# Routed experts of one mixture-of-experts layer: another order of the experts, and another way of adding the base

## The reference, cut to what matters

```
x = x + gnn(layernorm(x), edges)            # graph layer
xn = layernorm(x)
shared = sum over 2 shared experts:  silu(xn @ sWg[e]) * (xn @ sWu[e]) @ sWd[e]
gate = top 6 of 64 softmax(xn @ Wr), made to sum to 1, else 0
routed = sum over e in 0..63: (silu(xn @ Wg[e]) * (xn @ Wu[e]) @ Wd[e]) * gate[:, e]
out = x + (shared + routed + xn)            # all weights 512 x 512, f32
```

## Time and profile before

| | |
|---|---|
| median of 3 runs | 756.45 us (755.75 to 759.19) |
| the profiled execution, its own time | 754.59 us |
| its span, first to last instruction | 752.8 us |
| PE busy | 696.7 us (93%) |
| DVE, ACT, POOL busy | 251.4, 221.1, 174.0 us |
| DMA | 236.33 MB, 314 GB/s over the span |
| TensorE clock granted | 0.988 of full speed, mean |

### The profile page before, as it was taken

The page is one execution under the profiler, slowest core; times in us unless marked ns, Lnnn a source line. Parts: engine busy times, 40 slices in busy tenths (PEclk is TensorE's granted clock), DMA queues, the critical chain, the costliest instruction groups (busy, mean ns, idle before and its releaser), DMA issues. The chain is left out here.

```text
span 752.8 us, 17410 instructions
## 1 busy us (share of the span) xinstructions
PE 696.7 (93%) x6982; PEld 474.1 (63%) x6982; DVE 251.4 (33%) x795; ACT 221.1 (29%) x536; POOL 174.0 (23%) x157
## 2 busy tenths in 40 slices
PE   3689999899999999999999999999999999999960
PEld 2467777566766666555666666655567777777740
DVE  6975625775112432221212111122323222221000
ACT  5733323512332222212222222221222333233320
POOL 4000000012222322323322222223333332232202
PEclk9999999999999999999999999999999999999996
DMA  9925112447999999999999999999999999999962
GB/s 270 410 86 224 39 74 81 156 145 261 362 372 343 388 389 382 386 393 385 378 389 383 381 399 380 385 393 385 385 382 375 371 368 370 367 375 373 381 165 28
DMA packets 63408, 236.33 MB, mean 314 GB/s; under 512 B 7323, under 2 KB 7359, under 8 KB 51550
## 3 DMA queue, kind: packets, MB, share of 16 engines
q1 hardware_dynamic: 51764, 211.33, 73.3%
q0 software_dynamic: 10144, 20.56, 11.7%
q10 hardware_dynamic: 1418, 3.30, 1.2%
HBM read 222.32 MB, written 12.83 MB: 312 GB/s over the span
## 5 line engine op out<-in xcount | busy, mean ns | idle before, releaser
L461 POOL DMA_INDIRECT xg<-x_tab,idx_sb x64 | 69.9, 1092 | 375.5 <-DVE idx_sb L1048 193.6
L1528 PE MATMUL ps<-ring,xT 128*64 128x256 f32 x1296 | 148.4, 380 | 0.2 <-DVE hs L1107 0.2
L473 POOL DMA_INDIRECT out<-ysb,idx_sb x64 | 93.3, 1458 | 189.6 <-issue 112.7
L1528 PEld LDWEIGHTS ps<-ring,xT 128*64 128x64 f32 x1296 | 93.6, 137 | 46.7 <-issue 1.1
L1041 DVE TENSOR_REDUCE gates<-ps 128x1 f32<-128x3 f32 (+1 forms) x62 | 10.0, 162 | 331.3 <-PE ps L1434 330.6
L707 ACT ACTIVATE ysb<-ps 64x256 f32<-64x256 f32 x64 | 24.1, 377 | 201.4 <-PE ps L1528 192.9
L1528 PE MATMUL ps<-ring,hTj 128*64 128x256 f32 x624 | 76.0, 386 | 0.0
L1528 PE MATMUL ps<-w,xT 128*64 128x256 f32 x608 | 69.8, 379 | 0.4 <-DMA w<-in_L_ffn_Wu 0.4
L1009 DVE TENSOR_TENSOR onehot<-iotaAB,slotv 125x640 bf16<-125x640 f32 (+1 forms) x64 | 67.3, 1052 | 0.5 <-issue 0.3
L1528 PEld LDWEIGHTS ps<-ring,hTj 128*64 128x64 f32 x624 | 41.4, 136 | 28.7 <-issue 11.7
L1528 PEld LDWEIGHTS ps<-w,xT 128*64 128x64 f32 x608 | 44.3, 137 | 22.0 <-issue 0.8
(11 more groups left out here) (254 smaller groups left out, 819.2 us busy)
## 6 DMA issues: line engine op xcount, KB each, us to landing
ring<-in_L_ffn_Wd SPq DMA_DIRECT2D x39, 1024.0 KB, 18.5
ring<-in_L_ffn_Wg SPq DMA_DIRECT2D x27, 1024.0 KB, 19.3
ring<-in_L_ffn_Wu SPq DMA_DIRECT2D x27, 1024.0 KB, 17.6
w<-in_L_ffn_Wd SPq DMA_DIRECT2D x20, 1024.0 KB, 21.7
w<-in_L_ffn_Wg SPq DMA_DIRECT2D x14, 1024.0 KB, 14.9
ring<-in_L_ffn_Wg SPq DMA_DIRECT2D x28, 512.0 KB, 15.1
w<-in_L_ffn_Wu SPq DMA_DIRECT2D x13, 1024.0 KB, 20.4
ring<-in_L_ffn_Wu SPq DMA_DIRECT2D x26, 512.0 KB, 16.3
```

Of the source, the lines that this page charges most:

```text
L461: g.indirect_dma_start(out=xg[j % NX][0:ROWS[j], :], out_offset=None, in_=x_tab, in_offset=bass.IndirectOffsetOnAxis(ap=idx_sb[0:ROWS[j], ...
L473: g.indirect_dma_start(out=out, out_offset=bass.IndirectOffsetOnAxis(ap=idx_sb[0:ROWS[j], j:j + 1].bitcast(u32), axis=0), in_=ysb[j % NY][ ...
L1528: last = t_.matmul(ps[h * BIG:(h + 1) * BIG, bank, 0:AW], big(k), w[:, k, h * AW:(h + 1) * AW], start=(k == 0), stop=(k == KD - 1))
```

## The change

The change has three parts.

- **Order.** `RANK[j]` is j: places 0 to 21 are big and 22 to 63 small.
- **Shared units.** The 23 late units stand at places 22 to 57 and no longer at 6 to 46. With them the wait of PE for the list of extra tiles moves from place 14 to place 22.
- **Base.** Additions 0 to 60 go into `y_tab`, a table in DRAM that is filled with zeros in place of `out`. When addition 60 has landed, SP loads the table by plain DMAs into `fin` in SBUF (five tiles of 125x512, in the space of `xnT`, two DMAs each), POOL adds `x_sb` to each tile, and SP writes the sums to `out`. Additions 61, 62 and 63 go into `out` after the last of these has landed. All gathers stand ahead of the merge.

```
-    LAST = 1
-    RANK = (list(range(FIXED)) + list(range(NBIG, E - LAST)) + list(range(FIXED, NBIG)) + list(range(E - LAST, E)))
+    RANK = list(range(E))
     ROWS = [[r for a, r in ROW_STEPS if a <= rank][-1] for rank in RANK]
     CAPS = [CAP if rank < NBIG else BIG for rank in RANK]
-    BASE_AFTER = 59
+    MERGE_AFTER = 60
...
-        free = [j for j in range(FIXED, FIXED + E - LAST - NBIG) if j not in (SPREAD + 4, SPREAD + 5)]
+        free = list(range(NBIG, MERGE_AFTER - 1))
...
+            rows_of = out.rearrange("(t p) d -> p t d", p=P)
+            sums_of = y_tab.rearrange("(t p) d -> p t d", p=P)
+            sp.wait_ge(s_sy, NS * T)
+            sp.wait_ge(s_scat, 16 * (MERGE_AFTER + 1))
+            for t in range(T):
+                for a, b in PARTS:
+                    sp.dma_start(fin[a:b, t, :], sums_of[a:b, t, :]).then_inc(s_fin[t], 16)
+            for t in range(T):
+                sp.wait_ge(s_merged, t + 1)
+                for a, b in PARTS:
+                    sp.dma_start(rows_of[a:b, t, :], fin[a:b, t, :]).then_inc(s_out, 16)
...
-            g.dma_start(out[0:full * 128, :].rearrange("(t p) d -> p t d", p=128),
+            g.dma_start(y_tab[0:full * 128, :].rearrange("(t p) d -> p t d", p=128),
...
-                if j == BASE_AFTER + 1:
-                    pool.wait_ge(s_base, 32)
+                if j == MERGE_AFTER + 1:
+                    pool.wait_ge(s_out, 32 * T)
                 pool.sem_inc(s_go, 1)
-                g.indirect_dma_start(out=out,
+                g.indirect_dma_start(out=y_tab if j <= MERGE_AFTER else out,
...
-            def add_base():
+            def merge():
 
                 pool.wait_ge(s_sy, NS * T)
-                pool.wait_ge(s_scat, 16 * (BASE_AFTER + 1))
-                for a, b in PARTS:
-                    g.dma_start(out.rearrange("(t p) d -> p t d", p=P)[a:b, :, :], x_sb[a:b, :, :],
-                                accum_op=ALU.add).then_inc(s_base, 16)
+                for t in range(T):
+                    pool.wait_ge(s_fin[t], 32)
+                    g.tensor_tensor(fin[:, t, :], fin[:, t, :], x_sb[:, t, :], ALU.add).then_inc(s_merged, 1)
...
```

More of the change, by code:

```diff
@@ L193, in gnn_moe_kernel @@
         xnT = rHT.place("xnT", [128, KD, N], f32)
+        rHT.rewind()
+        fin = rHT.place("fin", [P, T, D], f32)
         w1 = [rRaw.place(f"w1_{i}", [128, KD, 512], f32) for i in range(2)]
@@ L253, in gnn_moe_kernel @@
         x_tab = nc.dram_tensor("x_tab", [N, D], f32, kind="Internal").ap()
+        y_tab = nc.dram_tensor("y_tab", [N, D], f32, kind="Internal").ap()
         def sem(name):
@@ L297, in gnn_moe_kernel @@
         s_scat = sem("y_added")
-        s_base = sem("base_added")
+        s_fin = [sem(f"sum_in{t}") for t in range(T)]
+        s_merged, s_out = sem("merged"), sem("out_written")
         W1v = W1.rearrange("(k p) n -> p k n", p=128)
@@ L336, in gnn_moe_kernel @@
         late = units[GAP + 1:]
-        free = [j for j in range(FIXED, FIXED + E - LAST - NBIG) if j not in (SPREAD + 4, SPREAD + 5)]
+        free = list(range(NBIG, MERGE_AFTER - 1))
         unit_at.update({free[i * len(free) // len(late)]: u for i, u in enumerate(late)})
         AFTER = min(j for j in unit_at if j > SPREAD + 5)
-        assert max(unit_at) < BASE_AFTER
+        assert max(unit_at) < MERGE_AFTER
         DT = 3
@@ L406, in _ @@
                     sp.dma_start(ring[2][:].rearrange("p (h b) n -> p h b n", h=2), down_pairs[e]).then_inc(s_ring[2], 16)
-            sp.wait_ge(s_base, 32)
+            sp.wait_ge(s_out, 32 * T)
             sp.wait_ge(s_scat, 16 * E)
@@ L438, in _ @@
             rest = full * 128 + EVEN
-            g.dma_start(out[0:full * 128, :].rearrange("(t p) d -> p t d", p=128),
+            g.dma_start(y_tab[0:full * 128, :].rearrange("(t p) d -> p t d", p=128),
                         zrows[:].unsqueeze(1).broadcast_to([128, full, D])).then_inc(s_pre, 16)
-            g.dma_start(out[full * 128:rest, :], zrows[0:EVEN, :]).then_inc(s_pre, 16)
-            g.dma_start(out[rest:N, :], zrows[0:N - rest, :]).then_inc(s_pre, 16)
+            g.dma_start(y_tab[full * 128:rest, :], zrows[0:EVEN, :]).then_inc(s_pre, 16)
+            g.dma_start(y_tab[rest:N, :], zrows[0:N - rest, :]).then_inc(s_pre, 16)
             g.memset(ones_f[:], 1.0).then_inc(s_cst, 1)
@@ L493, in _ @@
                 scatter(j)
-                if j == BASE_AFTER:
-                    for i in range(n, min(E, n + 1)):
+                if j == MERGE_AFTER:
+                    for i in range(n, E):
                         gather(i)
-                    n = min(E, n + 1)
-                    add_base()
+                    n = E
+                    merge()
             pool.wait_ge(s_scat, 16 * E)
```

## The result

The changed kernel takes 766.75 us (median of 4 runs, 765.83 to 769.52) against 757.62 for the one before (4 runs beside it, 755.75 to 759.19): a ratio of 1.0135, 95% interval 1.0115 to 1.0155. It is slower by 9 to 10 us, where no change was forecast. The profiled execution took 765.83 us with a span of 763.6 and a mean clock of 0.979; before it was 754.59 and 752.8.

A forecast was written before the change was run, and what follows sets the result against it. PE was taken to pace nearly all the routed stage, POOL's additions the end. Base start +12.5, base cost -6.1, later additions -6.3 made +0.1 us: 754.7, plus 1.86 to the median, 756.6 us; range 747.5 to 763.5.

The forecast's parts named there:

- The sum: Whole timeline from hs of place 22 at 368.3 to a span of 752.9 us, against 752.8 before.
- 747.0, and 5.9 to the end: End of the kernel: addition 63 issued at 747.0 us, the span ending 5.9 us later at 752.9.
- Order and units: Routed stage on PE: 9.40 us a big place, 6.30 a small one, last result at 728.2, 7.4 us earlier.
- 7.5 us to spare: Last six small places: weights keep a lead of about 7.5 us, so PE doesn't wait for them.
- The chain: POOL's additions, each waiting for the one before: 8.1 us apart from 57 on, addition 60 at about 720.2.
- eight times 0.8: Places 50 to 57: the additions' lag shrinks by 0.8 us a place, from 10.0 to about 3.8.
- The merge: After addition 60: SP loads from 725.0, five POOL adds of 1.2 us, writes landed at 737.2; 12.4 us in all.
- the 3 us I had put on that choice: Merge's adds: doing them on VectorE and not on GpSimd would be worth some 3 us.
- The chain did not keep up: Rival on additions 57 to 60: they come nearer to 5 than 8 us apart, giving 748.2 us; chance 0.27.
- the rival had 12.5 us of delay: Rival on the last small places: weights run out, PE waits, giving 763.7 us; chance 0.13.
- the merge was not dearer: Rival on the merge: adds of 1.87 us and landings of 3 us, not 2, giving 761.7 us; chance 0.10.

The follow-up runs named there:

- two tables: Changed kernel with additions alternating between two zero-filled tables, each its own chain, both summed with the base on VectorE after the last; 751.83 us, ratio 0.993.
- the order alone: Changed kernel with the accumulating base behind place 59 as before, in place of the merge; 757.98 us, ratio 1.001.

## Why the prediction was wrong

The sum against the trace, in us from the span's start:

```
                                   predicted   measured
hs of place 22                        368.3     369.27
hs of place 58                        687.5     688.42
hs of place 63                        719.0     720.53
last result                           728.2     729.38
addition 60                           720.2     719.87
SP's first load                       725.0     726.28
first addition of the merge           728.0     729.42
addition 61                           737.4     739.23
addition 63                           747.0     748.32
from it to the end of the span          5.9      15.3
```

- **The step that failed** is the last of the sum, "747.0, and 5.9 to the end". I took those 5.9 us from the old trace as if they belonged to the landing of an addition. The runs showed what they were: 3.7 of landing, 1.0 of reading and testing the overflow count, 0.967 of DRAIN and 0.2 of semaphores, and the DRAIN is 10.522 us in the changed kernel. The DRAIN depends on what GpSimd had issued before: the accumulating base was also the plain DMA that kept it short. The term was 9.4 us too small; all before it was 1.3 too early. Without the long DRAIN this execution would have had a span of about 754.1, and the sum said 752.9.
- **Order and units** were right to 1.5 us: 9.40 and 6.30 a place, the last result 6.3 us earlier than before (7.4 forecast). The weights had no 7.5 us to spare at the end but nothing, since PE waits 1.8 us there. Loads near 470 us landed in 15.5 to 18.1 us (medians), not in the 25.7 of the earlier trace rows.
- **The chain** was right in the last places, and not in the middle. The additions from 57 on are 7.7, 7.7 and 8.0 apart (8.1 taken), and their lag behind ACT's first copy grows 3.4, 4.9, 6.3, 8.0 against 3.8 to 9.2. In the middle the lag was 6.8 (place 38: copy at 529.78, addition at 536.54), not the 10.0 of the earlier trace rows. At that place it wasn't the chain that held the addition but the gather ahead of it, issued at 535.28 after a wait for its row numbers, as with two tables. The lag fell by 3.3 from place 49 to 57 (6.75 to 3.44) and not by eight times 0.8. The two errors cancelled, so the 3.8 forecast for place 57 came near by luck. The experiment with the order alone shows that additions and base take back all that the order gives, and the two tables show that in the last places it is the chain.
- **The merge** was right: five additions of 1.25 us (1.2 taken). The Trainium skill ("GPSIMD Engine Reference", elementwise accounting) gave 1.12 as an estimate, near to it. By the same page VectorE is about twice as fast, and the trace agrees with 0.69 us; but of the 3 us I had put on that choice only 0.7 was to be had, since the loads became the bound. Addition 61 was 1.8 later than forecast, 1.3 of it from SP's first load.
- **The rivals.** None holds. The chain did not keep up; PE waited 1.8 us for weights in the last steps, where the rival had 12.5 us of delay; the merge was not dearer. The time, above my range, came from a place that no case named. The expectation with an elementwise operation on GpSimd as the cause was wrong as well.

## What to carry to other kernels

What follows the last instruction is a term of its own, and it is not a constant: split it (landing, what the engine still reads, DRAIN) before carrying it over to a changed program, and look in the instruction queues' records when the span ends well after the last row. When the transfers of one engine form a chain, work saved ahead of the chain is lost in it; a second table with its own chain let the last 13 additions follow their results, and only then did the better order show in the time. A cost that stays in the program (here the DRAIN) may still be hidden, by letting the engine that pays it finish first.

## What the runs showed of the hardware

- GpSimd's DRAIN at the program's end lasts longer the more indirect DMAs it has issued since its last plain one: 0.885 us at 3, 0.967 at 4, 1.212 at 14, 1.783 at 21, 5.050 at 61 and 10.522 at 128, the same to the nanosecond in all five profiled executions with 128.
- Near the end, one addition comes later than its own result and the landing before it explain, in all nine kernels here in which GpSimd issues a plain DMA behind the fills, and in none of the five others. It is addition 62 in the kernel before (6.2 us after 61) and with the order alone (5.9), and 63 with the plain DMA ahead of the merge (7.45), where its neighbours are 4.5 to 4.9 apart. These three are each the third indirect DMA behind the plain one, but that isn't what counts: with the base behind place 50, it is addition 62 again, which starts 2.2 us after ACT's copy has ended, and addition 61 started 0.8 us after its own. Counted from the program's start, the late one is GpSimd's 132nd DMA in all of these, and its 129th (addition 60) with a plain DMA behind addition 30 or 54. The cause is open.
- An addition of two float32 tiles of 125x512 takes 1.25 us on GpSimd and 0.69 on VectorE.
- Additions into a table in DRAM that wait for each other go every 4.5 to 4.9 us with the DMA engines empty and every 7.3 to 8 while weights come at 380 GB/s.
